# Wide attention: routing spread over other units, and the next batch's keys and value rows ahead of the query and the tails

## What is computed

```
x = x + jnp.tanh(g_xattn[1]) * _L1_xattn_ref(_layernorm(x, axis=-1), ctx_1024, ctx_1024, L1_xattn_Wq, ...)
x = x + jnp.tanh(g_ffn[1]) * _L1_ffn_ref(_layernorm(x, axis=-1), L1_ffn_gate_w, L1_ffn_gate_up_w, L1_ffn_down_w)
```

## Time and profile before

| | |
|---|---|
| median of 3 runs | 1565.92 us (1562.40 to 1566.38) |
| the profiled execution | 1570.91 us, its span 1569.1 us |
| busy in the span | PE 1293.9 us (82%), DVE 948.7 (60%), ACT 722.1 (46%), POOL 532.2 (34%) |
| mean granted clock of TensorE | 0.896 of full speed |
| the wide attention's loop over units | about 331 to 572 us of the span |

### The profile page before, as it was taken

The page is one execution under the profiler, slowest core; times in us unless marked ns, Lnnn a source line. Parts: engine busy times, 40 slices in busy tenths (PEclk is TensorE's granted clock), DMA queues, the critical chain, the costliest instruction groups (busy, mean ns, idle before and its releaser), DMA issues. The chain is left out here.

```text
span 1569.1 us, 25219 instructions
## 1 busy us (share of the span) xinstructions
PE 1293.9 (82%) x8930; PEld 751.1 (48%) x8930; DVE 948.7 (60%) x2159; ACT 722.1 (46%) x1938; POOL 532.2 (34%) x625
## 2 busy tenths in 40 slices
PE   3799629879988859777996798989987978996998
PEld 2444317645555536454442455555654434442443
DVE  6466631355656754267564788878774865665664
ACT  3254413367756424343443565646664233453222
POOL 2320250545333252342001374747543320001443
PEclk8599859889999878895997899999988986998999
DMA  2455020240000011322000000000000001000000
GB/s 59 120 147 128 26 84 22 67 90 11 1 1 1 1 49 57 94 62 34 10 3 1 1 1 1 2 1 1 1 1 1 1 12 21 10 3 1 7 7 14
DMA packets 67134, 45.31 MB, mean 29 GB/s; under 512 B 17707, under 2 KB 60403, under 8 KB 67011
## 3 DMA queue, kind: packets, MB, share of 16 engines
q1 hardware_dynamic: 61155, 34.48, 8.5%
q0 software_dynamic: 4096, 8.40, 2.1%
q10 hardware_dynamic: 1760, 0.82, 0.3%
HBM read 24.91 MB, written 13.89 MB: 25 GB/s over the span
## 5 line engine op out<-in xcount | busy, mean ns | idle before, releaser
L3475 ACT ACTIVATE L2a_pr<-psum,L2a_negmax 128x512 f32<-128x512 f32 (+3 forms) x256 | 132.2, 531 | 94.2 <-DVE L2a_negmax L3601 40.2
L583 ACT ACTIVATE L1x_praw<-psum,L1x_negmax 128x154 f32<-128x154 f32 x256 | 96.2, 391 | 67.5 <-DVE L1x_negmax L708 67.4
L319 POOL TENSOR_TENSOR L1x_pm<-L1x_praw,L1x_total 128x1024 f32<-128x1024 f32 x32 | 60.7, 1898 | 144.6 <-DVE L1x_total L714 116.2
L3340 PE MATMUL psum<-ident,L2a_pr 128*128 128x128 f32 x640 | 85.9, 278 | 19.2 <-DVE L2a_pT L3614 11.8
L3340 PEld LDWEIGHTS psum<-ident,L2a_pr 128*128 128x128 f32 x640 | 71.7, 142 | 24.9 <-issue 21.2
L2042 POOL TENSOR_TENSOR L3f_scaled<-L3f_sg,L3f_wide 128x512 f32<-128x512 f32 (+1 forms) x44 | 55.8, 1272 | 66.8 <-ACT L3f_sg L2121 37.8
L1675 DVE TENSOR_REDUCE L3x_negmax<-psum 128x6 f32<-128x924 f32 (+1 forms) x48 | 47.7, 1012 | 46.7 <-PE psum L1213 37.4
L1675 DVE TENSOR_REDUCE L0x_negmax<-psum 128x6 f32<-128x924 f32 (+1 forms) x48 | 47.8, 1011 | 45.6 <-PE psum L1213 41.0
L3228 POOL TENSOR_TENSOR L2a_pr<-L2a_pr,L2a_total 128x768 f32<-128x768 f32 x32 | 48.6, 1520 | 69.9 <-DVE L2a_total L3630 69.6
L3225 POOL TENSOR_TENSOR L2a_pr<-L2a_pr,L2a_total 128x1024 f32<-128x1024 f32 x29 | 56.5, 1947 | 46.3 <-DVE L2a_total L3630 46.2
L708 DVE TENSOR_REDUCE L1x_negmax<-psum 128x4 f32<-128x616 f32 x64 | 50.8, 794 | 35.2 <-PE psum L389 32.4
(11 more groups left out here) (744 smaller groups left out, 3363.9 us busy)
## 6 DMA issues: line engine op xcount, KB each, us to landing
expert_arena<-in_L_ffn_w SPq DMA_DIRECT2D x16, 256.0 KB, 4.5
group_in<-zero SPq DMA_DIRECT2D x2, 1472.0 KB, 9.3
L1f_xs<-group_in SPq DMA_DIRECT2D x10, 256.0 KB, 4.1
group_out<-L1f_ys SPq DMA_DIRECT2D x10, 256.0 KB, 2.3
L1f_gu<-in_L_ffn_gate_up_w SPq DMA_DIRECT2D x8, 256.0 KB, 3.8
slots_in<-zero SPq DMA_DIRECT2D x1, 1280.0 KB, 9.1
L0f_xs<-slots_in SPq DMA_DIRECT2D x5, 256.0 KB, 4.2
resid<-in_x SPq DMA_DIRECT2D x4, 256.0 KB, 5.8
```

Of the source, the lines that this page charges most:

```text
L319: nc.gpsimd.tensor_tensor(pm[:, n % 2].rearrange("p j t k -> p (j t) k"), praw[:, n % 3, :, :, 0:MAIN].rearrange("p j t k -> p (j t) k"), ...
L583: nc.scalar.activation(praw[:, n % 3, j, t, :], psum[:, 2 * u + j, x * CTX:(x + 1) * CTX], ACT.Exp, bias=negmax[:, n % 2, u, j, x:x + 1], ...
L3340: last = nc.tensor.transpose(psum[:, TURN + n // 4, n % 4 * P:(n % 4 + 1) * P], pr[:, m % RING, n * P:(n + 1) * P], core.ident[:])
L3475: ins = nc.scalar.activation(pr[:, i % RING, SEQ * j + lo:SEQ * j + hi], psum[:, bank + j, lo:hi], ACT.Exp, bias=negmax[:, i % RING, e:e + ...
```

## The change

On PE, the pieces of the next batch in H0 and H1 now come right after `values`, ahead of the query and the tails; the tails come last in the round and wait for the copies out of H1 instead. ACT copies keys and turned values ahead of the query, and DVE copies value rows ahead of the tails. The routing begins sooner: `spread` in round 22 instead of 24, its root in 23 instead of 25, `front` one half in each of the rounds 23 and 24, the row transpositions in 24 and 25 in bank IN, logits in 26, the two `best` behind rounds 26 and 27 instead of 27 and 28, `ranks` in 28 and `place` in 28 instead of 29, `table` in 29 instead of 30. The scatters are issued two row tiles in each of the rounds 29, 30 and 31 and two behind the loop, instead of two in round 30 and six behind the loop. Parts 1 to 3 of finishing batch 2 move from rounds 27, 29 and 30 to 30, 32 and 33, and its root on ACT behind the loop.

```diff
--- before.py
+++ after.py
@@ -278,7 +278,7 @@
         got = sb("got", [P, 2 * QT * D])
         flat = praw[:].rearrange("p a j t k -> p (a j t k)")
         rows = got[:].rearrange("p (b t d) -> p b t d", b=2, d=D)
-        turned_rows = [core.x1[:].rearrange("p n d -> p (n d)")[:, 0:SEQ], xn[:, 1].rearrange("p t d -> p (t d)")]
+        turned_rows = [xnT[:], xn[:, 1].rearrange("p t d -> p (t d)")]
         results = [flat[:, 0:2 * QT * D], flat[:, 2 * QT * D:4 * QT * D], got[:], got[:]]
 
         def key_unit(i):
@@ -327,9 +327,10 @@
                     ins.then_inc(s["nt"], 1)
                     if n == 12:
                         grouped.constants(nc.gpsimd)
-                    if n == NS - 2:
-                        grouped.scatter(nc.gpsimd, 0, rows.rearrange("p b t d -> p (b t) d"), 0, 2)
-                grouped.scatter(nc.gpsimd, 0, rows.rearrange("p b t d -> p (b t) d"), 2, 2 * QT)
+                    if n >= NS - 3:
+                        t0 = 2 * (n - NS + 3)
+                        grouped.scatter(nc.gpsimd, 0, rows.rearrange("p b t d -> p (b t) d"), t0, t0 + 2)
+                grouped.scatter(nc.gpsimd, 0, rows.rearrange("p b t d -> p (b t) d"), 6, 2 * QT)
 
             @block.tensor
             def _(pe):
@@ -493,53 +494,54 @@
                             pe.wait_ge(s["vw"], 4 * b + (5, 7).index(g) + 1)
                         if n < NS and b >= 2 and g in (1, 2):
                             pe.wait_ge(s["vw"], 4 * (b - 1) + 2 + g)
-                        if b == B - 1 and g == 3:
-                            pe.wait_ge(grouped.s["xt"], 2)
-                        if b == B - 1 and g == 4:
-                            pe.wait_ge(grouped.s["lg"], 1)
-                        if b == B - 1 and g == 6:
-                            pe.wait_ge(grouped.s["rank"], 1)
                         turned(m)
                     if b and b < B and g == 3:
                         if follows:
                             pe.wait_ge(s["q"], n + NG)
+                        else:
+                            pe.wait_ge(grouped.s["lg"], 1)
                         rows_back(b - 1)
                     if 0 < n < NS:
                         scores(n, 1)
                     if 0 <= n - 3 < NS:
                         values(n - 3)
-                    if n < NS and follows:
+                    if n < NS and follows and g == 0:
                         pe.wait_ge(s["q"], n + NG)
-                        if b and g == 3:
-                            pe.wait_ge(s["yr"], b)
-                        if g == 0:
-                            rowsT(b + 1, IN)
-                        query(n + NG, IN)
-                    if n < NS and b == B - 1 and g in (2, 3, 5):
-                        pe.wait_ge(s["pt"], 2 * (n - 2) + 1)
-                        if g == 2:
-                            grouped.rowsT(pe, 0, rows[:, 0], H0)
-                        if g == 3:
-                            grouped.logits(pe, 0, turned_rows, H0)
-                        if g == 5:
-                            grouped.ranks(pe, 0, H0)
-                    if n >= 3 and n % 2 and n - 2 < NS:
-                        tails(n - 2)
+                        rowsT(b + 1, IN)
                     if n < NS:
                         if n >= 2:
                             pe.wait_ge(s["pt"], 2 * (n - 2) + 2)
-                        if b == B - 1 and g == 2:
-                            grouped.rowsT(pe, 1, rows[:, 1], H1)
                         if follows and g in (2, 5, 7):
                             keys(b + 1, (2, 5, 7).index(g), H0)
-                        if b and n % 2 and (follows and g in (3, 5) or b >= 2 and g == 1):
-                            pe.wait_ge(s["tt"], (n - 1) // 2)
                         if b and follows and g in (2, 3, 5):
                             values_turned(b + 1, (2, 3, 5).index(g), H1)
                         if b and follows and g in (4, 6):
                             values_out(b + 1, g // 2 - 2, H0)
                         if b >= 2 and g in (0, 1):
                             values_out(b, 2 + g, H0)
+                    if n < NS and follows:
+                        pe.wait_ge(s["q"], n + NG)
+                        if b and g == 3:
+                            pe.wait_ge(s["yr"], b)
+                        query(n + NG, IN)
+                    if b == B - 1 and g == 0:
+                        pe.wait_ge(s["q"], NS)
+                        grouped.rowsT(pe, 0, rows[:, 0], IN)
+                    if b == B - 1 and g == 1:
+                        pe.wait_ge(grouped.s["xt"], 1)
+                        grouped.rowsT(pe, 1, rows[:, 1], IN)
+                    if b == B - 1 and g == 2:
+                        grouped.logits(pe, 0, turned_rows, IN)
+                    if b == B - 1 and g == 4:
+                        pe.wait_ge(s["yr"], B - 1)
+                        grouped.ranks(pe, 0, IN)
+                    if n >= 3 and n % 2 and n - 2 < NS:
+                        if b and follows and g in (3, 5):
+                            pe.wait_ge(s["vt"], 3 * (b + 1) + (3, 5).index(g) + 2)
+                        if 2 <= b < B and g == 1:
+                            pe.wait_ge(s["vw"], 4 * b)
+                        tails(n - 2)
+                pe.wait_ge(grouped.s["rank"], 1)
                 rows_back(B - 1)
                 grouped.experts(pe, 0)
 
@@ -635,7 +637,7 @@
 
                 for n in range(NS):
                     b, g = n // NG, n % NG
-                    if b == B - 1 and g == 1:
+                    if n == NS - NG - 1:
                         grouped.spread_root(act, 0)
                     if n:
                         exps(n, 0)
@@ -643,22 +645,22 @@
                     if b + 1 < B:
                         if g == 0:
                             rowsT(b + 1, IN)
-                        query(n + NG, IN)
                         if g in (2, 5, 7):
                             keys(b + 1, (2, 5, 7).index(g), H0)
                         if b and g in (2, 3, 5):
                             values_turned(b + 1, (2, 3, 5).index(g), H1)
-                    if b == B - 1 and g == 2:
-                        for x in range(2):
-                            grouped.rows_out(act, x, turned_rows[x], (H0, H1)[x])
+                        query(n + NG, IN)
+                    if b == B - 1 and g in (0, 1):
+                        grouped.rows_out(act, g, turned_rows[g], IN)
                     if n == 6:
                         rows_root(2)
                     if n == 14:
                         rows_root(3)
                     if b and g == 2:
                         output(b - 1)
-                    if b and g == 4:
+                    if b and b + 1 < B and g == 4:
                         root(b - 1)
+                root(B - 2)
                 output(B - 1)
                 root(B - 1)
 
@@ -777,20 +779,15 @@
                         finished(b - 1, 0)
                     if 0 < n < NS:
                         maxima(n, 1)
-                    if n >= 3 and n % 2 and n - 2 < NS:
-                        tails(n - 2)
                     if n < NS:
                         if b and b + 1 < B and g in (4, 6):
                             values_out(b + 1, g // 2 - 2, H0)
                         if b >= 2 and g in (0, 1):
                             values_out(b, 2 + g, H0)
-                    if b and b < B and g >= 3:
-                        if g == 3:
-                            finished(b - 1, 1)
-                        if g == 5:
-                            finished(b - 1, 2)
-                        if g == 6:
-                            finished(b - 1, 3)
+                    if n >= 3 and n % 2 and n - 2 < NS:
+                        tails(n - 2)
+                    if b and b + 1 < B and g in (3, 5, 6):
+                        finished(b - 1, (3, 5, 6).index(g) + 1)
                     if n == 2:
                         summed(2)
                     if n == 7:
@@ -799,18 +796,20 @@
                         summed(3)
                     if n == 15:
                         normed(3)
+                    if n == NS - NG - 2:
+                        grouped.spread(0)
+                    if n in (NS - NG - 1, NS - NG):
+                        x = n - NS + NG + 1
+                        grouped.front(dve, v, x, rows[:, x])
                     if b == B - 1:
-                        if g == 0:
-                            grouped.spread(0)
-                        if g == 1:
-                            for x in range(2):
-                                grouped.front(dve, v, x, rows[:, x])
-                        if g in (3, 4):
-                            grouped.best(dve, v, 0, g - 3, H0)
+                        if g in (2, 3):
+                            grouped.best(dve, v, 0, g - 2, IN)
+                        if g == 4:
+                            grouped.place(dve, v, 0, IN)
                         if g == 5:
```

(4 more changed lines are left out.)

## The result

The changed kernel takes 1552.73 us (median of 5 runs, 1546.62 to 1554.50) against 1566.38 for the kernel before on the same chip (5 runs): the ratio is 0.9903, with a 95% interval of 0.9876 to 0.9930, a gain of 13.65 us between the medians. The ratio on record is not the quotient of the two medians (0.9913); by it the gain is 15.2 us. One of the five executions of the kernel before took 4832.86 us, a slow one that the ratio leaves out; without it the median of before is 1566.15 and the gain 13.4. The forecast was 1550, and faster.

The account below looks back on a forecast made before the run. TensorE sets the pace in batches 1 and 2, with short waits for late copies; in the last batch DVE's routing is in the way. Gains 2.3 + 2.9 + 2.3 + 8.5 = 16.0 take 1565.92 to about 1550 us, range 1543 to 1560.

Parts of the forecast that it names:

- Body: Batch 0, batches 1 and 2 and the start of batch 2: gains of 2.3, 2.9 and 2.3 us.
- last batch: From unit 24's transpositions to the end of the row transpositions: 75.5 us becomes 67.0, a gain of 8.5.
- Block end: Behind the row transpositions: finishing and loads all move with them, and the scatters stay ahead of both.
- Batches 1 and 2 without the start of batch 2: Recurring TensorE waits shrink by 1.6, 1.9 and 1.0 us, against 1.6 for the tails: gain 2.9.
- the start of batch 2: Waits of 2.8 us together are covered, 0.5 left for the tails behind the product at g = 1: gain 2.3.
- the wait of the tails for ACT at g = 5: Batches 1 and 2: tails that now come last wait for ACT, a loss of 0.6 us in all.
- The 0.87 at g = 3: Batches 1 and 2: this wait goes because turned value rows no longer stand behind the tails, 1.6 us in all.
- Batch 0: Keys ahead of query at g = 2: 0.6 us of wait, 0.8 of clock, about 0.9 of smaller waits: 2.3.
- POOL takes over the end: Last batch: three groups of scatters count in full, 15.2 us against about 4; whole gain 7.8, 1558 us; chance 0.15.
- Nothing net: Last batch: moved chains delay DVE in other units by their own length; gain 0.8, 1565 us; chance 0.10.
- Slower: Ten places: tails wait for their bank, then the next unit for their copy, 2.4 us each; 1573 us; chance 0.05.
- POOL held up by DVE: Eight scatter instructions ahead of the last product each wait for DVE, up to 22 us; 1572 us; chance 0.03.

Follow-up runs that it names:

- the second execution of before: The kernel before, unchanged, profiled once more in a single execution: 1565.03 us.
- the values first: Changed kernel with turned values ahead of the keys at g = 2 and 5, on TensorE and ACT: 1547.66 us, a single execution.
- the routing alone: Changed kernel with the old order of the round; routing, scatters and finishing of batch 2 as changed: 1557.20 us, ratio 0.9949 to the kernel before.
- scatters as before: Changed kernel with two tiles scattered in round 30 and six behind the loop: 1554.31 us, a single execution.
- all behind: Changed kernel with all eight tiles scattered behind the loop: 1549.37 us, a single execution.
- one tile: Changed kernel with one tile scattered in each of rounds 29 to 31, five behind the loop: 1544.99 us, ratio 0.9864 to the kernel before.
- both: Changed kernel with turned values ahead of keys, one tile in each of rounds 28 to 31, four behind: 1542.12 us, ratio 0.9835 to the kernel before.
- the order alone: Kernel before with only the order of the round changed; routing, scatters and finishing as before: 1562.21 us, ratio 0.9959.

## Why the prediction was right, and where it was not

The forecast held: 1552.73 lies 2.7 above it and inside the range. That the sum came so near is in part luck. Body and last batch were forecast at 7.5 and 8.5 and gave 6.6 and 8.2, or 5.0 and 6.6 beside the second execution of before, whose clock held better; a gain of 2.6 or 3.1 at the block's end, which the prediction put at nothing, made up for it. The steps, one by one:

**Last batch: right.** 67.0 us were forecast from unit 24 to the end of the row transpositions, and 67.25 measured. Units 24 and 25 took 14.38 (14.2), unit 26 6.93 (6.8), 27 5.39 (5.7), 28 6.15 (6.3), 29 5.49 (5.8), 30 5.25 (5.4), 31 5.99 (6.2), 32 7.57 (7.7). The two waits for POOL, forecast as 2 and 4, are 1.83 and 3.93, and a group of two tiles took POOL 4.87 (531.55 to 536.42; forecast 5.1). Only the rest was too low, 10.1 for 8.9: in this execution the clock fell right behind the wait, and both the transpositions (1.94) and the values (3.62) pay. That belongs to the execution and not to the change: the same stretch took 8.98 with the values first, behind the same wait of 3.93, and 7.30 with the routing alone, where the clock had fallen behind the wait before it.

**Block end: the step failed.** It said that the next stage "all moves with" the row transpositions, behind which DVE finishes and the experts' numbers are loaded, and so gave the scatters no price at the end. That they "stay ahead of both" is true of the changed kernel, where the last one ends 0.8 us behind the row transpositions; it was not true of the kernel before. The row that spoke against it was at hand: in the earlier trace rows DVE waits 3.91 us, where 1.21 is enough (the kernel after). The scatters already ended the block before, by about 2.7 us; the change takes POOL off the end, and 2.6 more was won than the row transpositions won. Nor do scatters cost nothing at the end in other divisions: with fewer scatters in the loop they end it again, by 5.6 and 8.1 us (DVE's waits of 6.76 and 9.27, less 1.21).

**Body: the sum nearly right, two terms wrong.** 7.5 was forecast and 6.6 measured (5.0 beside the second execution of before, where unit 3 alone is 1.6 shorter). Batches 1 and 2 without the start of batch 2 gave 2.4 (forecast 2.9), the start of batch 2 2.15 (2.3). The mis-sized term is the wait of the tails for ACT at g = 5: 0.3 each was forecast and 1.27 measured, because ACT's two table loads at g = 4 and the three copies of keys ahead of the right one were left out. Moving that copy alone gave 0.83 in each place. The tails' own cost was small: of the next unit's waits for their copy only 0.36 (unit 8) and 0.32 (unit 24) are noted, where 0.1 in ten places was counted. The 0.87 at g = 3 went as forecast: units 11 and 19 are shorter by 0.94 and 0.95, where 0.8 each was counted.

**Batch 0: the right size for the wrong reason.** Units 2 to 9 gained 2.04 (forecast 2.3), but not by a shorter wait. The 1.98 of the earlier trace rows has only been divided, 0.84 + 0.54 + 0.60 in the changed kernel: the keys, put ahead of the query, now wait for DVE to empty H0, which the query used to cover. Units 2 and 3 took 13.80 in the profile of before and 12.51 in the changed kernel; where the clock held with the old order (the routing alone, the kernel before once more) they took 12.23. So 1.6 us is clock that the first execution of before lost, the new order costs 0.3 where the clock holds anyway, and units 4 to 9 gave the other 0.75. Whether the shorter waits protect the clock is not settled: it fell here in one of three executions with the old order (the kernel before twice, the routing alone) and in none of seven with the new one.

**The rivals.** *POOL takes over the end* was the nearest: POOL does set TensorE's pace from unit 31 on, at a cost of 4.9 to 7.8 us. It did not give back the gain because the same scatters, had they stood behind, would have ended the block just as late. *Nothing net* fell: DVE is busy 5.20 of 5.39 us in unit 27 and 5.14 of 5.49 in unit 29 and in units 26 to 30 TensorE waits for it only once, 0.35. *Slower* by 2.4 in ten places fell by the rows above; tails do wait for their bank at g = 5 (1.27 twice) and at g = 1 (0.26 and 0.73, for DVE), but no wait for their own copy follows there. *POOL held up by DVE* fell: the scatters' mean is 995 ns beside 984 before, the longest 1.19, with DVE busy 17.4 of the 29.6 us from 526.5 to 556.1. The rule of the Trainium skill, page "SBUF — State Buffer", section "SBUF: two separate sides", would by that page's figures have cost 20 us, as an estimate; the longest of these scatters in any run here took 1.37 us. The section gives its figures for a DVE copy in a two-port mode, for which it names fp32 copies from SBUF to SBUF; DVE's copies beside these scatters read PSUM, so the rows speak against the price here and do not test that case.

## What to carry to other kernels

Where a block ends when every engine has left it, read how long each engine waits at its end: an engine that waits much longer than the shortest such wait seen (here 3.91 against 1.21) names another path that ends last, and here work on the first path alone won nothing. If one engine's work can stand either in the way of the pace-setter or at the end, neither extreme is best; deal it out until both paths end together (here one tile a round, four behind, 4.4 to 5.6 us better than two a round). And when a copy is moved ahead of another in an engine's queue, ask for each consumer which copy it waits for: the order of two copies was worth 0.83 us in each place.

## What the runs showed of the hardware that was not expected

The next stage starts 5.89 to 5.91 us after the start of the last scatter in five runs where POOL ends the block (the kernel before once more, scatters as before, all behind, one tile, both), and 6.13 in two more, the first profile of before and the order alone, whose last scatter took 1.19 instead of 0.95: from the end of the instruction it is about 4.94 in all seven. With one tile a round the view of DMA issues gives 2.2 us from issue to landing, the median of the last 13 scatters; what the rest consists of was not taken apart.

How far the clock falls behind a wait differs between executions of the same code: 0.77 of full speed in unit 3 of one execution of before and 1.00 in another, behind the same 1.98 us. The first of the two, from its table of stretches:

```profile
338.50:345.89 7.39, 7.33 (x34) 4.57 (x34) 4.99 (x16) 3.87 (x17) 2.53 (x3) 0.77 0.00 0
```

And a stage behind the change differs too, with the same code in it. The stretch from 142 to 200 us after the next stage's start, with one tile a round, and then in the version with both:

```profile
705.11:763.11 58.00, 55.37 (x556) 26.80 (x548) 38.47 (x67) 29.16 (x53) 5.03 (x4) 0.98 0.06 12
```

```profile
702.76:760.76 58.00, 56.13 (x478) 27.26 (x478) 34.86 (x55) 27.12 (x49) 5.03 (x4) 0.87 0.06 12
```

At 0.98 TensorE gets 556 matmuls done in the time of 478 at 0.87. From the next stage's start to the end of the program the one takes 978.5 us and the other 985.0, with the same code from there on; the two executions of before take 984.9 and 983.4, the changed kernel 981.1. So the 3.8 us that the two first profiles differ by behind the stage are within what executions differ by, and are not counted for the change.
